# Pieces of the projections and of the feed-forward on the two 64-row halves of the array, between two pairs of attention scores

## The reference, cut to what matters

```
xn = layernorm(x)
u, v, q, k = split(silu(xn @ W1 + b1), 4)               # W1: 256 x 1024; 16 heads of 16
attn = silu(q @ k.T) / 1024 ; av = attn @ v             # per head, 1024 x 1024 scores
y = layernorm(av * u) * gamma + beta ; y = y @ W2 + b2
h = layernorm(xn) * l1g + l1b ; h = gelu(h @ ternary(w1).T + fb1)   # 256 -> 1024
f = (layernorm(h) * l2g + l2b) @ ternary(w2).T + fb2                # 1024 -> 256
out = x + y + f
```

## Time and profile before

| | before |
|---|---|
| median of 3 runs | 1492.8 us (1492.14 to 1492.99) |
| the profiled execution, its time | 1493.36 us |
| its span, first to last instruction | 1491.6 us |
| PE busy | 1464.8 us, 98% |
| ACT busy | 1208.9 us, 81% |
| DVE busy | 895.3 us, 60% |
| POOL busy | 97.4 us, 7% |
| DMA | 83 GB/s mean |

### The profile page before, as it was taken

One profiled execution on the slowest core, in us unless ns is written; L12 is line 12 of the kernel. 1 busy time (PEld: TensorE's weight loads), 2 busy tenths in 40 slices (PEclk: granted clock), 3 DMA queues, 4 the chain that ended last, 5 costly groups with the idle time before them and its releaser, 6 DMA issues.

```text
span 1491.6 us, 25963 instructions
## 1 busy us (share of the span) xinstructions
PE 1464.8 (98%) x9942; PEld 784.7 (53%) x9942; DVE 895.3 (60%) x1719; ACT 1208.9 (81%) x1273; POOL 97.4 (7%) x197
## 2 busy tenths in 40 slices
PE   8999999999999999999999999999999999999998
PEld 7445555455554555554554455545555455554544
DVE  5557655576546854468654685447755476545745
ACT  4788888888788887887878878788788887888885
POOL 2001000010000100001000010000100001000001
PEclk9999999999999999999999999999999999999999
DMA  7351052410524106340153402443033510435100
GB/s 248 81 128 57 15 132 65 130 57 15 156 71 100 58 15 156 95 104 29 30 155 99 113 1 59 126 129 84 1 89 110 142 57 5 115 81 142 29 1 29
DMA packets 67996, 123.49 MB, mean 83 GB/s; under 512 B 12832, under 2 KB 14496, under 8 KB 66976
## 3 DMA queue, kind: packets, MB, share of 16 engines
q1 hardware_dynamic: 67712, 121.57, 29.9%
q10 hardware_dynamic: 160, 0.26, 0.1%
HBM read 79.84 MB, written 41.94 MB: 82 GB/s over the span
## 4 chain that ended last, share of the span: by engine, by line
PE 88%; DVE 5%; ACT 4%; issue 1%; DVEq 1%; DMA 0%; ACTq 0%
PE outs L1101 30%; PE scores L1079 22%; PE fill L1136 10%; PE fill L1170 9%; PE fill L1154 7%; PE fill L1186 3%; PE fill L1163 3%; ACT attn L636 3%; PE fill L1145 2%; DVE tmp L917 1%; PE fill L1126 1%; DVE hid L900 1%; ACT hid L681 1%; DVE st L813 1%; ACT L636 1%
## 5 line engine op out<-in xcount | busy, mean ns | idle before, releaser
L636 ACT ACTIVATE attn<-scores 128x1024 f32<-128x1024 f32 x1024 | 991.4, 1023 | 225.3 <-PE scores L1079 220.6
L1101 PE MATMUL outs<-attn,V 128*32 128x512 f32 x4096 | 494.3, 600 | 0.0
L1079 PE MATMUL scores<-QS,KS 64*128 64x512 f32 x2048 | 387.7, 452 | 8.3 <-ACT attn L636 7.0
L1079 PEld LDWEIGHTS scores<-QS,KS 64*128 64x128 f32 x2048 | 163.0, 184 | 300.4 <-ACT attn L636 241.5
L1101 PEld LDWEIGHTS outs<-attn,V 128*32 128x32 f32 x4096 | 107.2, 109 | 235.8 <-issue 235.1
L900 DVE SCALAR_TENSOR_TENSOR hid<-fill,ratq,fb1b 128x512 f32<-128x512 f32 x128 | 96.1, 751 | 77.6 <-PE fill L1154 72.3
L917 DVE TENSOR_TENSOR tmp<-fill,l2g 128x512 f32<-128x512 f32 x128 | 88.6, 692 | 88.6 <-PE fill L1163 81.1
L1170 PE MATMUL fill<-Wq,hgh 128*128 128x256 f32 x504 | 128.2, 292 | 2.0 <-DVE hgl L924 1.1
L1136 PE MATMUL fill<-xp,W1h 128*128 128x512 f32 x384 | 128.4, 416 | 0.5 <-DVE xp L949 0.5
L1170 PE MATMUL fill<-Wq,hgl 128*128 128x256 f32 x504 | 123.1, 282 | 0.0
L1170 PEld LDWEIGHTS fill<-Wq,hgh 128*128 128x128 f32 x504 | 95.8, 190 | 18.9 <-issue 14.6
(11 more groups left out here) (138 smaller groups left out, 1349.3 us busy)
## 6 DMA issues: line engine op xcount, KB each, us to landing
QS<-q_scratch SPq DMA_DIRECT2D x254, 128.0 KB, 3.3
k_scratch<-kst SPq DMA_DIRECT2D x64, 256.0 KB
q_scratch<-qst SPq DMA_DIRECT2D x64, 256.0 KB
KS<-k_scratch SPq DMA_DIRECT2D x128, 128.0 KB, 3.2
KS<-k_scratch SPq DMA_DIRECT2D x256, 64.0 KB, 3.4
out_dram<-part SPq DMA_DIRECT2D x15, 512.0 KB, 2.6
xin<-in_x SPq DMA_DIRECT2D x7, 1024.0 KB, 5.1
xin<-in_x SPq DMA_DIRECT2D x2, 512.0 KB, 4.3
```

Of the source, the lines that this page charges most:

```text
L636: nc.scalar.activation(attn_of(g)[:, 2 * hf:2 * hf + 2, :], SP[:, 2 * hf:2 * hf + 2, :], ACT.Silu).then_inc(s_silu, 1)
L1079: ins = mm(SP[:, j, :], KS[rows, pair, t * P:(t + 1) * P], QS[rows, pair - c * PPC, h * HALF:(h + 1) * HALF], start=True, stop=True)
L1101: ins = mm(OP[32 * j:32 * j + 32, g // RUN % 2, :], V[:, t, c * HPC // 2 + j, o * DH:o * DH + 2 * DH], attn_of(g)[:, n, :], start=(o == 0 ...
```

## The change

- **Scores are one call per half**, and PE's order in a round becomes: `times_v` of groups 2n-2 and 2n-1; both halves of the scores of group 2n+1; the first half of the round's first pieces; half 0 of the scores of group 2n+2; the second half of those pieces; half 1 of the scores of 2n+2; then what is left of the round. ACT follows: silu of both halves of 2n+1, steps ahead of the group, silu of half 0 of 2n+2, the other steps, silu of half 1.
- **Pieces in halves.** If the round has a k, u, f1, g or f2, its first such pieces (two, or one f2) are run with 64-row matmuls, two at a time, one in each half of the rows. k with q, u with u and f1 with f1 run crossed (`crossed`): in the first phase the upper rows go to one piece's bank and the lower rows to the other's, in the second the other way round, with a wait (`s_half`) for the first phase's end. g (`transposed`) makes 64-column transposes, tokens 0 to 63 in one bank and 64 to 127 in the other. f2 (`summed`) puts the sum of the upper rows in one bank and that of the lower rows in another, so it takes two banks and DVE adds twice. A g or f2 that follows in the same round runs in halves too; all other pieces run whole. Rounds with none of these kinds run their pieces whole between the scores of 2n+1 and of 2n+2. `lead` pieces (xt ahead of an f2) run whole ahead of the scores.
- **Banks.** `FP` has three banks, `OP` one.
- **The table is new**, and so are `OPENING` and `LAST_ROUNDS`. `k.1.0` no longer stands early in the first batch.

The core of the diff, first the new table, which replaces the old one of the same form:

```diff
+    "zs.0 zt.0 zs.1 zt.1",
+    "",
+    "",
+    "vs.1 a.0",
+    "",
+    "zt.2 zt.3",
+    "a.1 zs.2",
+    "",
+    "",
+    "zs.3 a.2",
+    "a.3 y.0",
+    "",
+    "",
+    "u.0",
+    "",
+    "kq.1.0",
+    "px y.2 u.1",
+    "",
+    "y.1",
+    "kq.1.1",
+    "f1.0",
+    "",
+    "f1.1",
+    "",
+    "y.3 gelu.0 f1.2 f1.3",
+    "f1.4",
+    "ln2.0 nrm2.0 f1.5",
+    "",
+    "",
+    "g.0",
+    "f1.6 f2.0 f1.7 gelu.1",
+    "gelu.2 g.1",
+    "",
+    "ln2.1 nrm2.1",
     "f2.1",
+    "",
+    "ln1 xn.0 g.2 ln2.2",
+    "",
+    "",
+    "xt.0",
+    "",
+    "f2.2 xn.1",
+    "g.3 nrm2.2",
+    "",
     "xt.1",
+    "f2.3",
+    "xn.2 g.4 xt.2",
+    "",
+    "f2.4 xn.3 gelu.3 g.5",
+    "v.0 ln2.3",
+    "xt.3 nrm2.3",
     "f2.5",
+    "",
+    "v.1",
+    "",
+    "kq.0.0 g.6",
+    "",
+    "v.2",
+    "",
+    "f2.6 v.3 g.7 vs.0",
+    "",
+    "kq.0.1",
+    "",
+    "f2.7",
...
+def pieces_of(b, n):
+    pieces = [xs for xs in steps_of(b, n) if xs[1][0] in FILLERS]
+    first = next((i for i, (x, s) in enumerate(pieces) if s[0] in GROUPED), len(pieces))
+    size = 0 if first == len(pieces) else 1 if pieces[first][1][0] == "f2" else 2
+    return pieces[:first], pieces[first:first + size], pieces[first + size:]
...
-        OP = ctx.enter_context(nc.psum_tensor("outs", [P, 2, HALF], F32))
-        FP = ctx.enter_context(nc.psum_tensor("fill", [P, 2, HALF], F32))
+        OP = ctx.enter_context(nc.psum_tensor("outs", [P, HALF], F32))
+        FP = ctx.enter_context(nc.psum_tensor("fill", [P, FILLS, HALF], F32))
...
+            def crossed(steps, phase):
+                if phase == 0:
+                    for x, step in steps:
+                        wait_free(x, step)
+                        wait_data(x, step)
+                else:
+                    pe.wait_ge(s_half, CROSSED.index(steps[0]) + 1)
...
             def body(b):
                 for n in range(ROUNDS):
-                    scores(b, 2 * n)
+                    lead, group, tail = pieces_of(b, n)
+                    halved, full = among_scores(b, n)
+                    nb, ng = next_group(b, 2 * n + 1)
                     for g in (2 * n - 2, 2 * n - 1):
                         if n:
                             times_v(b, g)
                         elif b:
                             times_v(b - 1, GROUPS + g)
-                    scores(b, 2 * n + 1)
-                    for x, s in steps_of(b, n):
-                        step(x, *s)
+                    if group:
+                        for x, s in lead:
+                            step(x, *s)
+                    for hf in range(2):
+                        scores(b, 2 * n + 1, hf)
+                    if not group:
+                        for x, s in lead:
+                            step(x, *s)
+                    for hf in range(2):
+                        if group:
+                            in_halves(group, hf)
+                        if nb < NB:
+                            scores(nb, ng, hf)
+                    rest = halved[len(group):]
+                    while rest:
+                        size = 2 if rest[0][1][0] == "g" else 1
+                        for phase in range(2):
+                            in_halves(rest[:size], phase)
+                        rest = rest[size:]
+                    for x, s in full:
+                        if group:
+                            step(x, *s)
```

More of the change, by code:

```diff
@@ L431, in last_piece @@
         def last_piece(bank):
-            return [xs for xs in PIECES if bank_of(*xs) == bank][-1]
+            return [xs for xs in PIECES if bank in [k for k, turn in BANKS[xs]]][-1]
         def last_a_tile(i, j):
@@ L1108, in warm_up, with wait_free, wait_data @@
                     mm(SP[:, 0, 0:P], ident[:, :], ident[:, :], start=True, stop=True)
+            def wait_free(x, step):
+                for k, turn in BANKS[x, step]:
+                    if turn > 1:
+                        pe.wait_ge(s_evac[k], turn - 1)
+            def wait_data(x, step):
+                kind, *a = step
+                if kind == "k" and a[0] == 0:
+                    wait_evacuated(pe, x, ("xt", 2 * a[1] + 1))
+                elif kind == "f1" and a[0] % 2 == 0 and a[1] == 0:
+                    pe.wait_ge(s_ht, NP * x + Y_ORDER.index(a[0] // 2) + 1)
+                elif kind == "g" and a[0] % 2 == 0 and a[1] == 0:
+                    pe.wait_ge(s_hn, NP * x + a[0] // 2 + 1)
@@ new lines, in summed @@
+            def summed(steps, phase):
+                (x, step), = steps
+                t = step[1]
+                if phase == 0:
+                    wait_free(x, step)
+                pe.wait_ge(s_hg, 2 * T * x + 2 * t + 2)
+                for n in range(4):
+                    for w in (hgh, hgl):
+                        for half, (k, turn) in enumerate(BANKS[x, step]):
+                            rows = slice(half * P // 2, (half + 1) * P // 2)
+                            ins = mm(FP[:, k, 0:D], w[rows, phase, n * P:(n + 1) * P], Wq2[rows, 4 * phase + n, :],
+                                     start=phase == 0 and n == 0 and w is hgh, stop=phase == 1 and n == 3 and w is hgl)
+                            if phase == 1 and n == 3 and w is hgl:
+                                ins.then_inc(s_fill[k], 1)
@@ L1280, in _ @@
                 step(0, *s)
+            for hf in range(2):
+                scores(0, 0, hf)
             for b in range(NB):
                 body(b)
-            pe.wait_ge(s_z, DC * NH * (NB - 1) + 3)
+            wait_evacuated(pe, *last_piece(2))
             last_hidden(0)
```

320 lines of the change are left out of this document (182 added, 138 removed).

## The result

| | before | after |
|---|---|---|
| median of 4 runs | 1492.65 us (1492.14 to 1492.99) | 1535.7 us (1532.22 to 1536.74) |
| ratio | | 1.0285, 95% interval 1.0267 to 1.0302 |
| the profiled execution, its time | 1493.36 us | 1532.22 us |
| its span | 1491.6 us | 1530.4 us |
| first scores / scores of the last group | 32.1 / 1479.0 us | 31.5 / 1517.9 us |

A forecast was written before the change was run, and what follows sets the result against it. PE, busy 98% of the span, bounds the kernel. Work left 167.1, floor 11.3 and waits 4.8 make 183.2 us a batch against 181.2; over eight batches 16.6 is added to 1493.4, giving 1510 us, range 1468 to 1532.

The forecast's parts named there:

- The floor: Rounds with too little PE work: scores, silu, scores, silu, then V take 4.82 us; 11.3 us a batch lost.
- its signs of being right: Rounds 14, 16, 18, 21, 23 each 4.82 us, no 0.1 gap before halved pieces, named bank waits, a batch of 183.
- Changes of shape dropped: Halved pieces share the scores' stretch in 23 of 32 rounds, saving 4.8 us a batch; 16 rounds without whole pieces save 3.0.
- pairs at the price of whole matmuls: In halved pieces, eight 128-row matmuls become eight pairs of 64-row ones, each pair costing one whole matmul.
- The third rival: Slower: in long runs pairs' loads aren't hidden, 0.108 more a pair outside g, 1694 us; chance 0.07 shared with another rival.
- The rule of the Trainium skill: On PE, weight loads overlap matmuls in flight only where they address other rows; against long runs of pairs, 1694 us.
- Waits for banks and for DVE: PE waits for readers of banks in rounds 15, 22, 24, 25, 27 and small ones: 4.8 us a batch.
- First and last batch are taken like the others: Batches at both ends were given the same 2.0 us more a batch as the rest.
- the gelus cost nothing: Gelus' 1.28 + 3.71 + 1.28 on ACT stand in rounds 12, 15 and 24, which have 8.3 to 10.7 of PE work.
- The first rival: Faster: bank and DVE waits don't bind, 178.4 a batch, 1471 us; chance 0.25 in full or most part (below 1490).

The follow-up runs named there:

- the second reordering: Changed kernel with, in the last batch, ln2.3 and nrm2.3 behind f2.5 (nrm2.3 just behind zt.1) and zs.1 ahead of g.6: 1528.3 us, ratio 1.0238.
- the three mended places together: Changed kernel with f2.0, g.5 and g.6 whole, the last batch's steps reordered and six unread matmuls in round 16: 1515.9 us, ratio 1.0151.
- the kernel with a busy round 16: Changed kernel with six more matmuls of the scores' shape in round 16, results read by nobody: 1532.2 us, ratio 1.0268.
- the four steps: From the kernel before to the change: banks 1492.6 to 1488.7, new table to 1519.4, scores of 2n+2 among the pieces to 1573.4, halves to 1535.7 us.
- V in the gap: Changed kernel with, in six rounds, group 2n's product with V moved between the two halves of the scores of 2n+2: 1546.8 us, ratio 1.0367.
- the kernel with f2 ahead: Changed kernel with both halves of an f2 that is a round's first piece run ahead of half 0 of the next scores: 1525.7 us, ratio 1.0214.

## Why the prediction was wrong in size and right in direction

The profiled execution came to 1532.2 where the sum said 1510.0: 22.2 us. Two steps of the forecast failed, by about as much: the one that took the last batch like the others (10.1 us), and the size of the waits (9.5 us in batches 1 to 6). The clock, which had no term, is 5.3 us, half of it inside the last batch. By batches, each forecast at +2.07: batch 0 has +2.8; batches 1 to 6 together +24.5 for 12.4; the last +12.2 for 2.1; the two ends, put at nothing, have -0.7. The steps one by one account for it; what a single round "was put at" is added up here from the forecast's terms:

- **The floor: right.** 4.82 us, its parts and its rounds. Rounds 0 to 5, 14, 18, 19, 26 and 28 have 4.81 to 4.82; round 12 was put at 8.87 and has 8.92, round 29 at 7.59 and has 7.59, rounds 21 and 23 at 5.38 and have 5.41. (The forecast contradicts itself here: its signs of being right say 4.82 for rounds 16, 21 and 23. They have 5.05, 5.41 and 5.41; rounds 21 and 23, as they are cut here, hold a whole xt beside their g, and the 5.38 that the forecast uses in its waits has it in.) The kernel with whole pieces keeps the same 4.82 in the rounds without a group.
- **Changes of shape dropped, and pairs at the price of whole matmuls: right.** Pairs 0.23 apart; halved pieces 0.57 behind the scores (651.91 to 652.48) for a forecast of 0.56; 38 us from halving. The third rival would have had 0.108 more for each pair. The rule of the Trainium skill (TensorE: Matmul & The Clock Gate, Part 3, what overlaps and what doesn't) would have had that too, and the rows of round 27 speak against it as those of before did.
- **Waits for banks and for DVE: right in place, too small.** This is the second step that failed. A plain batch takes 184.8 us (184.7 to 185.0 in the four of batches 1 to 6 without half clock) for a forecast of 183.2. If all of the 1.6 us is put to the waits, their 4.8 us a batch should have been some 6.4. The rounds: 24 has 9.17 for 8.83, 27 has 7.28 for 7.03, 15 has 10.91 for 10.73, 25 has 6.12 for 5.96, 16 has 5.05 for 4.90; against them round 30 has 5.84 for 6.02. One part that was missing is the way from one engine to the next, for which the sum had no term. DVE's last part of g.4 ends at 728.94 + 0.69 = 729.63, and f2.4 starts 0.15 later; DVE's first addition ends at about 732.90 (half of its 1.06), and g.5 starts 0.10 later; ACT has read k at 753.27, and g.6 starts 0.14 later. 0.10 to 0.15 us on each of some eight waits a batch comes to 0.8 to 1.2 us, an estimate from these three. It doesn't fall evenly: f2.0 of round 15 starts 4.02 after the scores for a forecast of 3.98 and f2.4 1.24 for 1.26, but g.6 4.78 for 4.63. The rest isn't apportioned; part of it is in rounds 6 to 9, which take 5.85 to 5.95 where the forecast's terms give 5.78 and for which the table above has no wait for a reader. No run separates these parts.
- **"First and last batch are taken like the others": wrong for the last.** This is the first step that failed: +12.2 for 2.1. `LAST_ROUNDS` is a table of its own, and the forecast walked only the other. Read in the same way (f2.5's reader behind nrm2.3 behind POOL), it would have shown the wait; the second reordering took back 6.5 us of it. Nor does "the gelus cost nothing" hold there: round 24 has 7.55 us in place of 9.17, and 1.90 of waiting for ACT follow. With the three mended places together, and no half clock, the last batch is 2.7 us above the kernel before, near the 2.1 of the forecast. For the first it held well enough: +2.8, where plain batches have +3.7.
- **The clock: no term.** Two stretches of 3.4 us at half clock in batches 1 and 5 make them 1.3 us longer each than their neighbours, 2.6 in all, and the 6.8 us at half clock in the last batch are 2.7 of its 12.2: in the kernel with a busy round 16, whose V behind the same wait runs at full clock, round 25 takes 11.07 for 13.24 and round 26 takes 4.82 for 5.36. The median is 3.5 us above the profiled execution, whose mean granted clock is 0.994, while the other three have 0.992 and 0.993; more of these stretches fit that, but no timeline of those executions shows it.
- **The first rival's sign** (waits don't bind, 1471) is out. The rows of waits above that aren't for `attn` and not of the last batch alone make 32.1 us, 4.0 a batch as idle time, where that rival decided at 2.8.
- **The range** ended at 1532, which took in 0.9 us a batch of more waits, and neither a last batch of its own nor the clock.

What the forecast did not ask, and the four steps show, is what the *table* costs by itself: it counted the floor only in the new order. In the old order the table alone, with the openings and last rounds that belong to it, costs 31 us.

## What to carry to other kernels

Gathering work to save the cost of switching empties other places; price the loop that those places fall back to (here scores, silu, scores, silu: 4.82 us) before the saving, and count how many fall on it. Every table has its own last and first rounds; walk each of them, step by step and queue by queue, or give them a range of their own. And when a step on a shared engine is moved to free one reader, look first at who needs its result: three times here (g.6, f2 behind V in the gap, g.2) the wait went on to the next need and took back most of what was won, or more.

## What was not expected of the hardware

**Short stretches of idle time bring the clock down.** In round 16 of batch 1 PE had 0.88 and 0.41 us of idle time ahead of the halves of the scores and 0.16 ahead of V, and V ran at half clock; in batch 3 the idle times are the same to the hundredth, and V ran at full clock:

```profile
317.56 0.50 PE L1148 MATMUL scores<-QS,KS 64*128 64x512 f32 x2 [0.88 <-ACT attn L680]
...
318.48 0.51 PE L1148 MATMUL scores<-QS,KS 64*128 64x512 f32 x2 [0.41 <-ACT attn L680]
...
319.14 3.01 PE L1166 MATMUL outs<-attn,V 128*32 128x512 f32 x16 [0.16 <-DVE uz L892]
...
688.35 0.50 PE L1148 MATMUL scores<-QS,KS 64*128 64x512 f32 x2 [0.88 <-ACT attn L680]
...
689.93 1.92 PE L1166 MATMUL outs<-attn,V 128*32 128x512 f32 x16 [0.16 <-DVE uz L892]
```

So the same round costs 5.05 or 6.1 us from one batch to the next. The engine had been doing the same beforehand in both; what decides between them no run here shows. That the gaps are needed for it is shown by more than one pair: in the eight kernels of the new table without the six extra matmuls, 20 of the 64 rounds 16 have a stretch at half clock and take 5.95 to 6.76 us (from one in the kernel with f2 ahead to four in others); in the two kernels with them none of 16. A round on the floor can thus cost more than its idle time. Whether this is also what spreads the executions is open: they lie 4.5 us apart for the change and 0.9 for the kernel before, but also 6.3 for the three together, whose profiled execution has no such stretch.

**Halved transposes cost a little over half.** The 16 of g.5 are eight pairs; at 0.72 us from first start to last end, with a last record of 0.22 us, a pair takes (0.72 - 0.22) / 7.5 = 0.07 (the last start is that of the second half of the eighth pair), for which the forecast took half of 0.108.
